# Second feed-forward of a two-layer attention block: the down product in three rounded parts, interleaved over four tiles

## The chip, the cores and the metric

The kernel runs on one core of a Trainium2 chip. Its engines are TensorE (PE: matmuls, with weight loads beside them), VectorE (DVE), ScalarE (ACT), GpSimd (POOL) and the DMA queues, here mostly issued by SyncE (SP). Each engine works through its own queue in order, and they wait for each other by semaphores. The metric is the device time of one execution in microseconds (us), the median of several runs.

## The reference, cut to what matters

`x` is 16 x 64 rows of 256 columns. Four residual stages follow one another: banded attention, a feed-forward on the chosen half of the rows, a cross attention with 32 query and 8 key heads, and the second feed-forward, which is the one that the change is about:

```python
def _L1_ffn_ref(hidden_states, gate_w, up_w, down_w, expert_weight, ln_gamma, ln_beta):
    logits = jnp.einsum('bsh,he->bse', hidden_states, gate_w)          # 8 logits
    routing_weights, selected_experts = jax.lax.top_k(logits, 2)
    h = jnp.einsum('bsh,hi->bsi', hidden_states, up_w)                 # 256 -> 1024
    h = jnp.square(jax.nn.relu(h))
    shared_out = jnp.einsum('bsi,ih->bsh', h, down_w)                  # 1024 -> 256
    y = shared_out + (hidden_states @ expert_weight) * routing_weights.sum(axis=-1, keepdims=True)
    mu = y.mean(axis=-1, keepdims=True)
    var = jnp.mean(jnp.square(y - mu), axis=-1, keepdims=True)
    return (y - mu) * jax.lax.rsqrt(var + EPS) * ln_gamma + ln_beta
x = x + _L1_ffn_ref(_layernorm(x), ...)
```

All is float32.

## The kernel before, in words

The 1024 rows are eight tiles of 128. The last part of the program, from the second half of the first feed-forward to the end of the cross attention, is written by hand as slots, `slot1(n)` for n from -18 to 53: every engine has a function of that name, and `at(n, first, step, count)` says which index of a job falls to slot n. Within a slot an engine does its jobs in the order of the code. Cross attention scores fall to slots 0 to 31 (L628), one (tile, quarter) a slot; the exponentials (L998 on ACT) and their products follow five and more slots later. A tile t of the attention ends with the output product at slot 14 + 4t (L684), its add into `x` on DVE at 15 + 4t (L1415), statistics at 17 + 4t, POOL's inverse deviation (`inv_std`, L1055 and L1058: add and power) and DVE's normalisation (L1209) at 18 + 4t, PE's transposes at 20 + 4t (L731) and the two halves of the normalised tile at 21 + 4t: a rounded copy on ACT (L992) and the rest, DVE's subtraction from it (L1384). With high and low halves of both operands a float32 product is made of three one-pass products (type fp32r): high x high, high x low, low x high. A plain float32 product is recorded as two instructions and takes more passes.

The second feed-forward works on halves of four tiles (512 rows). For each of 8 chunks f of the hidden width:
- PE `moe_up(half, f)` (L752): six fp32r products of 512 columns into bank `S[m % 2]`, m = 8 half + f. Called an up block below.
- ACT `moe_relu(m)` (L1015): relu from the bank into one of two buffers.
- the square: DVE `moe_square` (L1462) in the first half, POOL (L1193) in the second, into `hT`.

For each tile: PE's gate block (L771), six fp32r products of 264 columns for the expert product and the logits; DVE's top-two and their sum (L1468, L1470); ACT's scaling by that sum, `moe_scale` (L1024); PE's down product (L777), eight float32 products of 256 columns into a bank of `ST`, tile after tile; then on DVE, in `moe_out`, one behind another: the add (L1473), two statistics instructions (L1204, L1206), subtract the mean and multiply (L1477), wait for POOL's add and power (L1055, L1058), and the last multiply and add (L1482); SP stores the tile. POOL adds the residual and beta (L1184) in the tail.

In the first half, up blocks fall to slots 35 to 42, relu and square to 36 to 43, gate and down products to 44 to 51, half a tile a slot; `MOE_OUT` puts the closing of tiles 0 to 2 in slots 46, 48 and 53. After the slots PE does up blocks 8 to 15 and then gate and down product for tiles 4 to 7; DVE does `moe_out` for tiles 3 to 7.

The weights `up` and `down` (1 MB each) come with the other late loads at the start. ACT casts `up` into its high half at slots 29 to 32 (L977) and POOL subtracts (L1154) at 30 to 33; the gate weights follow at 37 and 38 (L980, L1157).

Of the kernel before, what the change touches and what calls it, by code (L numbers as in the profile page):

```python
# [23 lines left out]
P = 128  # L24
# [5 lines left out]
DF = 1024  # L30
# [18 lines left out]
def build(nc, a):  # L49
    ctx = ExitStack()  # L50
    with ctx:
# [6 lines left out]
        def sem(name):  # L58
# [36 lines left out]
        up = sb("up", [P, 2, DF])  # L95
        down = sb("down", [P, FC, T])
# [56 lines left out]
        names = ("ld_first ld_ctx ld_ctx2 ld_w0 ld_b0 ld_ident act_w0 pool_w0 act_part pe_part dve_part ld_small ld_x1 ld_x ld_rest ld_late st_out "  # L153
# [7 lines left out]
                 "h_ln h_rstd h_xn hp_xT ha_xT hl_xT ha_w hpool_w hpool_up h_xb hp_up ha_up h_up hp_dn hp_eg h_tk h_moe h_ln2 h_rstd2 h_y h_out").split()  # L161
# [75 lines left out]

        def stacked(p, i):

            return r32(q1[:, p % 3, :, :, :, i, :].rearrange("p g t b q -> p g (t b) q"))  # L240
# [12 lines left out]
        MOE_OUT = {46: 0, 48: 1, 53: 2}  # L253
# [58 lines left out]
        def _(sp):  # L312
            def load(dst, src, name):
# [28 lines left out]
                    (up[:, :, :], a["up"].rearrange("(k p) f -> p k f", p=P)),  # L342
                    (down[:, :, :], a["down"].rearrange("(k p) f -> p k f", p=P)),
                    (eg[:, :, 0:T], a["ew"].rearrange("(k p) f -> p k f", p=P)),
                    (eg[:, :, T:T + NEXP], a["gw"].rearrange("(k p) f -> p k f", p=P))]
            assert len(late) == 9
# [14 lines left out]
        LATE = 16 * 9  # L361
# [3 lines left out]
        def _(pe):  # L365
# [235 lines left out]
            def slot1(n):  # L601
# [154 lines left out]
            def moe_down(t, f0, f1):  # L756

                half, m = divmod(t, 4)
                if f0 == 0:
                    if t == 0:  # L760
                        pe.wait_ge(s["ga_o"], TILES)
                        pe.wait_ge(s["ga_ex"], 4 * TILES)
                    if t == 1:
                        pe.wait_ge(s["ga_hq"], PAIRS)
                        pe.wait_ge(s["g_lq"], PAIRS)
                    if t >= 2:
                        pe.wait_ge(s["h_y"], 2 * t - 3)
                    if t == 0:
                        pe.wait_ge(s["hpool_w"], 5)
                    for i, (k, a, b) in enumerate(PARTS):  # L770
                        last = mm((O, PJ)[t % 2][:, 0:T + NEXP], r32(xq[half][:, m, b, k, :]), r32(eg2[:, a, k, :]),  # L771
                                  start=(i == 0), stop=(i == len(PARTS) - 1))
                    last.then_inc(s["hp_eg"], 1)
                for f in range(f0, f1):
                    if m == 0:
                        pe.wait_ge(s["hpool_up" if half else "h_up"], f + 1)
                    last = mm(ST[t % 2][:, 0:T], hT[:, f, P * m:P * m + P], down[:, f, :], start=(f == 0), stop=(f == FC - 1))  # L777
                if f1 == FC:
                    last.then_inc(s["hp_dn"], 1)
# [12 lines left out]
        def _(act):  # L792
# [145 lines left out]
            def slot1(n):  # L938
# [31 lines left out]
                t = MOE_OUT.get(n)  # L970
                if t is not None:
                    moe_scale(t)
                i = at(n, 29, 1, 4)
                if i is not None:
                    act.wait_ge(s["gp_st"], 24)
                    k, c = divmod(i, 2)
                    nc.scalar.copy(r32(up2[:, 0, k, 512 * c:512 * c + 512]), up[:, k, 512 * c:512 * c + 512]).then_inc(s["ha_w"], 1)  # L977
# [620 lines left out]
```

## Time and profile before

| | |
|---|---|
| median of 3 runs | 342.35 us (341.98 to 342.72) |
| the profiled execution | 340.92 us |
| its span, first to last instruction | 339.2 us |
| PE busy | 307.2 us, 91% |
| PE weight loads | 239.0 us, 70% |
| DVE busy | 236.2 us, 70% |
| ACT busy | 199.6 us, 59% |
| POOL busy | 181.8 us, 54% |
| mean granted TensorE clock | 0.998 |

The profile is of one execution; times in it count from its first instruction. Busy times are of engines, and weight loads lie beside matmuls. A line such as L752 is a line of the kernel before. The chain is what ended last, followed back step by step to what released each step. The granted clock is the share of 2.4 GHz that PE was given. Matmuls are pipelined, so one that is recorded with 0.38 us can follow another after 0.22: counts over a stretch are read, not single durations.

### The profile page before, as it was taken

How to read it: one execution, taken by the hardware profiler on the slowest of the kernel's cores; microseconds unless marked ns; L12 is line 12 of the kernel's file. 1: busy time of each engine (PE TensorE's matmuls, PEld its weight loads, DVE VectorE, ACT ScalarE, POOL GpSimd, SP SyncE). 2: the span in 40 equal slices, each digit the busy share in tenths (PEclk: the TensorE clock that was granted, in tenths of full speed). 3: DMA queues.
4: the chain of work that ended last, by engine and by line, in shares of the span. 5: the costliest groups of instructions: out<-in, count | busy, mean ns of one | idle time of the engine just before them, and what ended most of it. 6: DMA issues, size and time to landing. Idle time of an engine off the chain costs nothing.

```text
span 339.2 us, 7193 instructions
## 1 busy us (share of the span) xinstructions
PE 307.2 (91%) x2166; PEld 239.0 (70%) x2166; DVE 236.2 (70%) x921; ACT 199.6 (59%) x414; POOL 181.8 (54%) x294
## 2 busy tenths in 40 slices
PE   1987999999999999999898998869899999999993
PEld 1966667777676767776587886647567677988892
DVE  6777788999999998984526346665788746661264
ACT  3757987878787888777640334376778953113210
POOL 5667565676785946585712712453342822335643
PEclk9999999999999999999999999999999999999999
DMA  7999010101010110100000000000000000000000
GB/s 188 366 371 332 3 44 7 46 3 41 12 33 15 25 25 19 32 2 4 2 0 0 0 2 0 0 2 1 2 1 2 0 2 0 3 31 15 18 31 31
DMA packets 13301, 14.51 MB, mean 43 GB/s; under 512 B 2512, under 2 KB 11984, under 8 KB 13264
## 3 DMA queue, kind: packets, MB, share of 16 engines
q1 hardware_dynamic: 12688, 13.72, 13.0%
q8 instruction: 19, 0.31, 0.4%
q10 hardware_dynamic: 576, 0.33, 0.3%
q14 instruction: 18, 0.15, 0.1%
HBM read 10.64 MB, written 1.05 MB: 34 GB/s over the span
## 4 chain that ended last, share of the span: by engine, by line
PE 61%; DVE 17%; issue 8%; ACT 6%; POOL 5%; DMA 1%; SPq 0%; POOLq 0%; DVEq 0%; ACTq 0%
PE S L752 6%; PE S L418 6%; PE O L445 5%; PE ST L429 4%; DVE masked L1251 4%; PE ST L777 4%; PE S L554 4%; PE S L628 2%; PE S L695 2%; PE PJ L672 2%; PE O L709 2%; PE XB L527 2%; PE PJ L383 2%; PE PJ L393 2%; PE XB L684 2%
## 5 line engine op out<-in xcount | busy, mean ns | idle before, releaser
L1251 DVE CUSTOM_DVE_ANT_0 masked<-S,band 128x192 bf16<-128x192 f32 x256 | 80.3, 353 | 14.1 <-PE S L418 13.0
L870 ACT ACTIVATE ex<-ST 128x384 f32<-128x384 f32 x128 | 61.4, 489 | 14.6 <-PE ST L429 12.6
L1055 POOL TENSOR_SCALAR rstd<-mv 128x1 f32<-128x1 f32 x40 | 12.0, 301 | 79.9 <-DVE mv L1206 79.8
L418 PE MATMUL S<-qk 128*128 128x384 f32 x128 | 53.4, 417 | 0.1
L429 PE MATMUL ST<-qk 128*128 128x192 f32 x256 | 47.7, 269 | 2.2 <-ACT ex L870 1.9
L429 PEld LDWEIGHTS ST<-qk 128*128 128x128 f32 x256 | 45.0, 189 | 4.5 <-issue 3.5
L1113 POOL TENSOR_SCALAR_AFFINE_SELECT ex<-ex 128x512 f32<-128x512 f32 x32 | 21.3, 665 | 30.3 <-ACT ex L870 30.1
L418 PEld LDWEIGHTS S<-qk 128*128 128x128 f32 x128 | 24.1, 188 | 17.3 <-issue 15.3
L445 PE MATMUL O<-ex,v 128*32 128x192 f32 x512 | 34.1, 338 | 0.0
L1393 DVE TENSOR_REDUCE mw<-S 128x8 f32<-128x512 f32 x32 | 21.9, 686 | 13.0 <-PE S L628 13.0
L840 ACT ACTIVATE hs<-PJ,sb,byhead 128x512 fp32r<-128x512 f32 x29 | 22.6, 779 | 12.5 <-PE PJ L384 12.0
L777 PE MATMUL ST<-down,hT 128*128 128x256 f32 x128 | 28.9, 379 | 0.0
L777 PEld LDWEIGHTS ST<-down,hT 128*128 128x128 f32 x128 | 23.8, 190 | 2.9
L1058 POOL TENSOR_TENSOR rstd<-rstd,given 128x1 f32<-128x1 f32 x40 | 23.0, 575 | 3.3
L752 PE MATMUL S<-qk 128*128 128x512 f32 x96 | 24.3, 402 | 0.0
L998 ACT ACTIVATE ex<-ST 128x512 f32<-128x512 f32 x32 | 19.1, 597 | 6.9 <-PE ST L641 6.3
L1251 DVE DVE_READ_ACCUMULATOR2_ANT mw<- 128x1 f32 x256 | 21.1, 82 | 0.0
L1015 ACT ACTIVATE cxT<-S 128x512 f32<-128x512 f32 x16 | 9.6, 598 | 19.4 <-PE S L752 19.4
L752 PEld LDWEIGHTS S<-qk 128*128 128x128 f32 x96 | 17.7, 188 | 4.3 <-issue 0.4
L1140 POOL TENSOR_TENSOR qk<-kp,kmask 128x512 fp32r<-128x512 f32 x16 | 16.5, 1056 | 7.7 <-PE ST L641 4.0
L1110 POOL TENSOR_SCALAR_AFFINE_SELECT ex<-ex 128x512 f32<-128x512 f32 x32 | 20.5, 642 | 0.0
L383 PE MATMUL PJ<-xs,w0h 128*128 128x256 f32 x58 | 18.2, 335 | 1.8 <-issue 1.5
(200 smaller groups left out, 709.2 us busy)
## 6 DMA issues: line engine op xcount, KB each, us to landing
qk<-kp SPq DMA_DIRECT2D x48, 48.0 KB
w<-in_w SPq DMA_DIRECT2D x2, 1024.0 KB, 10.0
cx<-in_cx SPq DMA_DIRECT2D x1, 1024.0 KB, 9.2
up<-in_up SPq DMA_DIRECT2D x1, 1024.0 KB, 11.6
down<-in_down SPq DMA_DIRECT2D x1, 1024.0 KB, 11.6
out<-x SPq DMA_DIRECT2D x8, 128.0 KB, 1.7
cxT<-in_cxT SPq DMA_DIRECT2D x1, 768.0 KB, 6.7
x<-in_x SPq DMA_DIRECT2D x1, 768.0 KB, 8.5
```

The source lines that it names most:

```text
L383: mm(bank[:, T * b:T * b + T], r32(w0h[:, n, :]), r32(xs[:, b, :]), start=True, stop=False)
L418: mm(out, r32(qp[:, t % 2, g, b, P * c:P * c + P]), r32(mv_), start=True, stop=True).then_inc(s["pe_s"], 1)
L429: last = mm(ST[n % 2][:, WIN * h:WIN * h + WIN], r32(kb[:, t % 2, g, 2 * w + h, b, P * c:P * c + P]), r32(qp[:, t % 2, g, b, BAND * c:BAND ...
L445: last = mm(O[32 * j:32 * j + 32, BAND * c:BAND * c + WIN], v0f[:, t % 2, c, b, j, 16 * g:16 * g + 32], ex[:, (n // 2) % 4, j, :], start=( ...
L752: last = mm(S[m % 2][:, :].rearrange("p (t c) -> p t c", t=4), r32(up2[:, a, k, P * f:P * f + P]), r32(xq[half][:, :, b, k, :]), start=(i ...
L777: last = mm(ST[t % 2][:, 0:T], hT[:, f, P * m:P * m + P], down[:, f, :], start=(f == 0), stop=(f == FC - 1))
L840: A(r32(hs[:, m % 2, :]), proj_bank(t, n)[:, :], ACT.Identity, bias=sb0[:, n:n + 1], scale=part0[:, n // 2:n // 2 + 1])\
L870: A(ex[:, (n // 2) % 4, 2 * w:2 * w + 2, :], ST[n % 2][:, 0:2 * WIN].rearrange("p (h k) -> p h k", h=2), ACT.Exp, scale=SCALE).then_inc(s[ ...
L1058: G.tensor_tensor(rstd[:, t:t + 1], rstd[:, t:t + 1], cols[:, 2:3], ALU.pow).then_inc(s[done], 1)
L1113: G.affine_select(out=e[:, :, 0:128], in_=e[:, :, 0:128], compare_op=ALU.is_ge, fill=0.0, base=0, pattern=[[0, 4], [1, 128]], channel_mult ...
L1251: last = V.tensor_tensor_reduce(out=masked[:, n % 2, h, :], in0=S[n % 2][:, WIN * h:WIN * h + WIN], in1=band[:, c, :], scale=1.0, scalar=N ...
L1393: V.tensor_reduce(rows.rearrange("p (i c) -> p i c", i=2)[:, :, 0:4], S[0][:, :].rearrange("p (i j k) -> p i j k", i=2, j=4), AX, ALU.max) ...
```

## The change

It touches the second feed-forward alone.

- **Down product.** `down` is split into a rounded half and the rest (`down2`; ACT at slots 13, 17, 21, 25, POOL at 14, 18, 22, 26). Each chunk of hidden values is split too: ACT squares the relu into a rounded half, DVE squares it in full and subtracts the rounded half. They lie in a ring of four buffers made of older tensors. The product of a tile and a chunk is three fp32r products of 256 columns.
- **Chunk by chunk.** `moe_down(tiles, f)` does chunk f for four tiles side by side. In the first half it falls to slots 39 to 46, two tiles sharing a bank. In the second half chunks 0 to 3 lie between up blocks, and chunks 4 to 7 are done tile after tile; gate blocks are a function of their own.
- **Closing in three stages.** `moe_top`, `moe_sum`, `moe_out` of different tiles are interleaved on DVE, with slots of their own and a written order after the slots.
- **Loads.** `up` and `down` are loaded into the first feed-forward's weight tensors once those are free.
- **POOL.** The squares of the second half leave it; the additions of beta move from the tail to slots 19 + 4t.

```diff
-        up = sb("up", [P, 2, DF])
-        down = sb("down", [P, FC, T])
+        down2 = sb("down2", [P, 2, FC, T])
...
+        def h_part(b, m):
+            i = m % 4
+            if b:
+                return kp[:, i, :, :].rearrange("p b k -> p (b k)") if i < 2 else w0l[:, i - 2, :, :].rearrange("p a b -> p (a b)")
+            return spread[:, i, :, :].rearrange("p a b -> p (a b)") if i < 2 else hs[:, i - 2, :]
+        def moe_sum_bank(t):
+            return ST[t // 2][:, T * (t % 2):T * (t % 2) + T] if t < 4 else (XB, MT, ST[0], ST[1])[t - 4][:, 0:T]
+        def ring_free(m):
+            last = m - 4
+            if last == FC - 1:
+                return s["hp_dn"], 4
+            return s["hp_df"], last + 1 if last < FC else last
...
-        MOE_OUT = {46: 0, 48: 1, 53: 2}
+        MOE_SCALE = {46: 0, 47: 1, 52: 2}
...
+            sp.wait_ge(s["fp_up"], 2 * FC)
+            load(w1[:, :, :], a["up"].rearrange("(k p) f -> p k f", p=P), "ld_up")
+            sp.wait_ge(s["fp_dn"], 4)
+            load(w2[:, :, :], a["down"].rearrange("(k p) f -> p k f", p=P), "ld_down")
...
PE, in slot1
-                i = at(n, 44, 1, FC)
-                if i is not None:
-                    moe_down(i // 2, 4 * (i % 2), 4 * (i % 2) + 4)
+                f = at(n, 39, 1, FC)
+                if f is not None:
+                    moe_down(range(4), f)
+                t = at(n, 44, 1, 4)
+                if t is not None:
+                    moe_gate(t)
...
+            def moe_gate(t):
...
+                if t >= 2:
+                    pe.wait_ge(s["h_moe"], t - 1)
...
+            def moe_down(tiles, f):
+                m = FC * (tiles[0] // 4) + f
+                pe.wait_ge(s["h_up"], m + 1)
+                if m == 0:
+                    pe.wait_ge(s["hpool_d"], 4)
+                    pe.wait_ge(s["ga_ex"], 4 * TILES)
+                if m == FC:
+                    pe.wait_ge(s["g_x"], TILES)
+                    pe.wait_ge(s["h_y"], 8)
+                for t in tiles:
+                    rows = slice(P * (t % 4), P * (t % 4) + P)
+                    for i, (a, b) in enumerate(((0, 0), (1, 0), (0, 1))):
+                        last = mm(moe_sum_bank(t), r32(h_part(b, m)[:, rows]), r32(down2[:, a, f, :]),
+                                  start=(f == 0 and i == 0 and (t >= 4 or t % 2 == 0)), stop=(f == FC - 1 and i == 2), skip_group_check=True)
+                    if f == FC - 1:
+                        last.then_inc(s["hp_dn"], 1)
+                if f < FC - 1 and len(tiles) == 4:
+                    last.then_inc(s["hp_df"], 1)
...
PE, after the slots
-            for f in range(FC):
-                moe_up(1, f)
-            for t in range(4, TILES):
-                moe_down(t, 0, FC)
+            second = range(4, TILES)
+            for f in range(3):
+                moe_up(1, f)
+            for f in range(3, FC):
+                if f < 7:
+                    moe_down(second, f - 3)
+                else:
+                    moe_gate(4)
+                moe_up(1, f)
+            moe_gate(5)
+            for t in second:
+                for f in range(4, FC):
+                    moe_down((t,), f)
+                if t + 2 < TILES:
+                    moe_gate(t + 2)
...
ACT
+                i = at(n, 13, 4, 4)
+                if i is not None:
+                    act.wait_ge(s["ld_down"], 16)
+                    nc.scalar.copy(r32(down2[:, 0, 2 * i:2 * i + 2, :]), w2[:, 2 * i:2 * i + 2, :]).then_inc(s["ha_d"], 1)
...
             def moe_relu(m):
                 act.wait_ge(s["hp_up"], m + 1)
                 if m >= 2:
+                    act.wait_ge(s["h_sq"], m - 1)
                 A(relu(m), S[m % 2][:, :], ACT.Relu).then_inc(s["ha_up"], 1)
+                if m == 0:
+                    act.wait_ge(s["gp_e"], 4 * PAIRS)
+                if m >= 4:
+                    act.wait_ge(*ring_free(m))
+                act.wait_ge(s["ha_up"], m + 1)
+                A(r32(h_part(0, m)), relu(m), ACT.Square).then_inc(s["ha_hi"], 1)
...
             for m in range(FC, 2 * FC):
                 moe_relu(m)
-                if m == FC + 3:
+                if m == FC:
                     moe_scale(3)
             for t in range(4, TILES):
                 moe_scale(t)
...
POOL
+                i = at(n, 14, 4, 4)
+                if i is not None:
+                    pool.wait_ge(s["ha_d"], i + 1)
+                    fs = slice(2 * i, 2 * i + 2)
+                    G.tensor_tensor(r32(down2[:, 1, fs, :]), w2[:, fs, :], down2[:, 0, fs, :], ALU.subtract).then_inc(s["hpool_d"], 1)
+                t = at(n, 19, 4, TILES)
+                if t is not None:
+                    pool.wait_ge(s["g_x"], t + 1)
+                    if t == 0:
+                        pool.wait_ge(s["fp_dn"], 4)
+                    G.tensor_tensor(with_beta(t), x[:, t, :], vecs[:, 4, :], ALU.add).then_inc(s["h_xb"], 1)
...
+            for t in range(TILES):
                 inv_std(t, "h_ln2", 2 * t + 2, "h_rstd2")
...
DVE
+                if n in (46, 47, 51):
+                    moe_top({46: 0, 47: 1, 51: 2}[n])
+                if n in (48, 50):
+                    moe_sum((n - 48) // 2)
+                if n in (49, 51):
+                    moe_out((n - 49) // 2)
...
+                V.tensor_tensor(squared(m), relu(m), relu(m), ALU.mult).then_inc(s["h_sq"], 1)
+                dve.wait_ge(s["ha_hi"], m + 1)
+                dve.wait_ge(s["h_sq"], m + 1)
+                if m == 0:
+                    dve.wait_ge(s["gpool_k"], 2 * TILES)
+                V.tensor_tensor(r32(h_part(1, m)), squared(m), h_part(0, m), ALU.subtract).then_inc(s["h_up"], 1)
...
-            for t in range(3, TILES):
-                moe_out(t)
+            moe_square(FC)
+            moe_sum(2)
+            moe_top(3)
+            moe_out(2)
+            moe_square(FC + 1)
+            moe_sum(3)
+            moe_out(3)
+            for m in range(FC + 2, 2 * FC):
+                moe_square(m)
+            moe_top(4)
+            moe_top(5)
+            for t in range(4, TILES):
+                moe_sum(t)
+                if 6 <= t + 2 < TILES:
+                    moe_top(t + 2)
+                if t >= 5:
+                    moe_out(t - 1)
+            moe_out(TILES - 1)
```

`moe_top(t)` is the top-two and their sum; `moe_sum(t)` waits for the scaled expert product and the tile's down product and does the add, the statistics and the subtract-and-multiply (it signals `h_y` after the add and after the last); `moe_out(t)` waits for POOL's power and does the last step.

## Rows read from the trace of the kernel before

**Rows 1.** The page's chain that ended last, shares by engine

```profile
PE 61%; DVE 17%; issue 8%; ACT 6%; POOL 5%; DMA 1%; SPq 0%; POOLq 0%; DVEq 0%; ACTq 0%
```

**Rows 2.** Windows: us, busy us (instructions) of each engine, granted clock, DMA share, GB/s

```profile
core 0: us, PE busy (x) PEld busy (x) DVE busy (x) ACT busy (x) POOL busy (x), PEclk, DMA share, GB/s
240.00:250.00 10.00, 8.81 (x69) 6.08 (x68) 7.90 (x17) 6.58 (x13) 5.57 (x7) 1.00 0.01 2
...
316.50:333.20 16.70, 16.70 (x89) 14.81 (x87) 8.57 (x23) 2.02 (x4) 8.97 (x15) 1.00 0.08 25
333.20:339.20 6.00, 0.11 (x1) 0.00 (x0) 2.32 (x8) 0.47 (x1) 1.08 (x2) 0.90 0.13 44
```

**Rows 3.** The chain in order of time, 260 to 340 us: start, us, what

```profile
276.50 0.22 PE XB L678 x2
276.72 0.57 PE O L709 x8
...
288.70 0.73 PE O L771 x6
289.43 3.45 PE ST L777 x16
...
297.29 0.74 PE O L771 x6
...
305.66 9.58 PE S L752 x42
...
318.34 0.68 POOL on L1184
```

**Rows 4.** Timeline of PE, 270 to 340 us: start, us, engine, line, what

```profile
296.90 0.38 PE L731 MATMUL MT<-ident,xn 128*128 128x128 f32 x2
...
305.31 11.28 PE L752 MATMUL S<-qk 128*128 128x512 f32 x48
...
329.70 3.62 PE L777 MATMUL ST<-down,hT 128*128 128x256 f32 x16
```

**Rows 5.** Timeline of DVE, 286 to 340 us; in brackets idle time and its releaser

```profile
332.43 0.84 DVE L1482 SCALAR_TENSOR_TENSOR x<-yr,rstd,on 128x256 f32<-128x256 f32 x1 [0.86 <-POOL rstd L1058]
333.20 0.16 DVE L1468 MAX8 tk<-PJ 128x8 f32<-128x8 f32 x1
333.39 0.16 DVE L1470 TENSOR_TENSOR rk<-tk 128x1 f32<-128x1 f32 x1
334.09 0.42 DVE L1473 TENSOR_TENSOR yr<-ST,onT 128x256 f32<-128x256 f32 x1 [0.54 <-ACT onT L1024]
...
335.01 0.18 DVE L1206 BATCH_NORM_AGGREGATE mv<-st 128x2 f32<-128x6 f32 x1
335.23 0.48 DVE L1477 SCALAR_TENSOR_TENSOR yr<-yr,mv,vecs 128x256 f32<-128x256 f32 x1
336.58 0.48 DVE L1482 SCALAR_TENSOR_TENSOR x<-yr,rstd,on 128x256 f32<-128x256 f32 x1 [0.86 <-POOL rstd L1058]
```

**Rows 6.** Timeline of ACT, 286 to 340 us

```profile
307.09 0.60 ACT L1015 ACTIVATE cxT<-S 128x512 f32<-128x512 f32 x1 [5.23 <-PE S L752]
...
333.58 0.47 ACT L1024 ACTIVATE onT<-PJ,rk 128x256 f32<-128x256 f32 x1 [3.67 <-DVE rk L1470]
```

**Rows 7.** Timeline of POOL, 286 to 340 us

```profile
332.27 0.72 POOL L1184 TENSOR_TENSOR on<-x,vecs 128x256 f32<-128x256 f32 x1
```

**Rows 8.** Weight loads of the gate block: ns min/median/max, first and last start

```profile
L771 PEld LDWEIGHTS O<-qk x24: 187/188/192, 288.4 to 325.3; 128*128 128x128 f32 x24
```

**Rows 9.** Groups by form, 180 to 340 us, ACT, POOL, DVE: busy us, mean ns

```profile
L977 ACT CAST qk<-up 128x512 fp32r<-128x512 f32 x4 | 2.5, 616 | 0.0
L992 ACT CAST qk<-MT 128x256 fp32r<-128x256 f32 x8 | 3.0, 372 | 0.8 <-PE MT L731 0.7
...
L1154 POOL TENSOR_TENSOR qk<-up,qk 128x512 fp32r<-128x512 f32 x4 | 5.1, 1273 | 2.9 <-ACT qk L977 2.9
...
L1462 DVE TENSOR_TENSOR hT<-cxT 128x512 f32<-128x512 f32 x8 | 5.5, 687 | 0.0
```

**Rows 10.** DMA issues: KB, median us from issue to landing

```profile
down<-in_down SPq DMA_DIRECT2D x1, 1024.0 KB, 11.6
```

**Rows 11.** Score products of slots 0 to 31: ns, first and last start us

```profile
L628 PE MATMUL S<-qk x64: 278/283/472, 208.1 to 265.1; 128*128 128x256 f32 x64
```

More of the change, by code:

```diff
@@ L754, in moe_up @@
                 last.then_inc(s["hp_up"], 1)
-            def moe_down(t, f0, f1):
+            def moe_gate(t):
                 half, m = divmod(t, 4)
[L759 to L779, printed above, removed]
@@ new lines, in moe_gate @@
+                if t == 0:
+                    pe.wait_ge(s["ga_o"], TILES)
+                    pe.wait_ge(s["hpool_w"], 5)
+                if t == 1:
+                    pe.wait_ge(s["ga_hq"], PAIRS)
+                    pe.wait_ge(s["g_lq"], PAIRS)
+                if t >= 2:
+                    pe.wait_ge(s["h_moe"], t - 1)
+                for i, (k, a, b) in enumerate(PARTS):
+                    last = mm((O, PJ)[t % 2][:, 0:T + NEXP], r32(xq[half][:, m, b, k, :]), r32(eg2[:, a, k, :]),
+                              start=(i == 0), stop=(i == len(PARTS) - 1))
@@ new lines, in moe_gate @@
+                last.then_inc(s["hp_eg"], 1)
+            def moe_down(tiles, f):
[16 more added lines that the diff above has]
+                    last.then_inc(s["hp_df"], 1)
@@ L1153, in slot1 @@
                     cs = slice(512 * c, 512 * c + 512)
[L1154 removed]
+                    G.tensor_tensor(r32(up2[:, 1, k, cs]), w1[:, k, cs], up2[:, 0, k, cs], ALU.subtract).then_inc(s["hpool_w"], 1)
+                i = at(n, 14, 4, 4)
[6 more added lines that the diff above has]
+                    pool.wait_ge(s["g_x"], t + 1)
+                    if t == 0:
+                        pool.wait_ge(s["fp_dn"], 4)
+                    G.tensor_tensor(with_beta(t), x[:, t, :], vecs[:, 4, :], ALU.add).then_inc(s["h_xb"], 1)
                 if n == 38:
@@ L1174, in _ @@
                 slot1(n)
-            def moe_norm(t):
-                pool.wait_ge(s["g_x"], t + 1)
-                if t == 0:
-                    pool.wait_ge(s["gp_bt"], TILES)
-                if t >= 2:
-                    pool.wait_ge(s["h_out"], t - 1)
-                G.tensor_tensor(on[:, t % 2, :], x[:, t, :], vecs[:, 4, :], ALU.add).then_inc(s["h_xb"], 1)
-                inv_std(t, "h_ln2", 2 * t + 2, "h_rstd2")
-            for t in range(3):
-                moe_norm(t)
-            for f in range(FC):
-                pool.wait_ge(s["ha_up"], FC + f + 1)
-                if f == 0:
-                    pool.wait_ge(s["hp_dn"], 4)
-                G.tensor_tensor(hT[:, f, :], relu(FC + f), relu(FC + f), ALU.mult).then_inc(s["hpool_up"], 1)
-            for t in range(3, TILES):
-                moe_norm(t)
+            for t in range(TILES):
+                inv_std(t, "h_ln2", 2 * t + 2, "h_rstd2")
         @block.vector
@@ L1470, in moe_out, with moe_sum @@
                 V.tensor_tensor(rk[:, t:t + 1], tk[:, t % 2, 0:1], tk[:, t % 2, 1:2], ALU.add).then_inc(s["h_tk"], 1)
+            def moe_sum(t):
+                y, scaled = moe_rows(t)
                 dve.wait_ge(s["h_moe"], t + 1)
-                dve.wait_ge(s["hp_dn"], t + 1)
-                V.tensor_tensor(yr[:, 0, :], ST[t % 2][:, 0:T], onT[:, t % 2, :], ALU.add).then_inc(s["h_y"], 1)
+                dve.wait_ge(s["hp_dn"], t + 1 if t >= 4 else t + 2 - t % 2)
+                if t == 1:
+                    dve.wait_ge(s["gp_bt"], TILES)
+                V.tensor_tensor(y, moe_sum_bank(t), onT[:, t % 2, :], ALU.add).then_inc(s["h_y"], 1)
                 dve.wait_ge(s["h_y"], 2 * t + 1)
-                stats(t, yr[:, 0, :], "h_ln2", 2 * t)
+                stats(t, y, "h_ln2", 2 * t)
                 dve.wait_ge(s["h_ln2"], 2 * t + 2)
-                V.scalar_tensor_tensor(out=yr[:, 1, :], in0=yr[:, 0, :], scalar=mv[:, t, 0:1], in1=vecs[:, 3, :],
+                V.scalar_tensor_tensor(out=scaled, in0=y, scalar=mv[:, t, 0:1], in1=vecs[:, 3, :],
                                        op0=ALU.subtract, op1=ALU.mult).then_inc(s["h_y"], 1)
+            def moe_out(t):
                 dve.wait_ge(s["h_y"], 2 * t + 2)
@@ L1486, in _ @@
                 slot1(n)
-            for t in range(3, TILES):
-                moe_out(t)
+            moe_square(FC)
[16 more added lines that the diff above has]
+            moe_out(TILES - 1)
 def constants():
```

30 lines of the change are left out of this document (15 added, 15 removed).

## Prediction

> **What bounds the kernel now.** I read the page's chain first: TensorE (PE) holds 61% of the chain that ended last, VectorE (DVE) 17% [rows 1]. Then the windows: from 316.5 to 333.2 us, the second half of the second feed-forward, PE has no idle time at all, at a granted clock of 1.00, its level of 2.4 GHz [rows 2]. The chain in order of time says what it does there: a gate block of six matmuls takes 0.74, a tile's sixteen half-passes of the fp32 down product 3.45, and 42 matmuls of the up product 9.58, so 1.37 for an up block of six [rows 3]. From 318.34 on the chain leaves PE: the closing steps of tile 3 and then of tiles 4 to 7 run one behind another on DVE, ScalarE (ACT) and POOL, about 4.14 a tile. That is as long as PE's gate and down work for a tile (0.74 + 3.45), so neither leads by much: PE's last matmul ends at 333.32 [rows 4], the last tile's sum starts on DVE at 334.09 [rows 5].
>
> The last tile also gives the price of the closing steps [rows 5 to 7]. Top-two: 333.20 to 333.55, 0.35. ACT's scaling: 0.47. Stage "sum" (add, two statistics, subtract and multiply): 334.09 to 335.71, 1.62. POOL's variance and power, from the statistics' end to the last step's start: 1.39. Last step: 0.48. From PE to ACT it takes about 0.4 beyond the block: the up block that starts at 305.31 leaves PE after 1.37 and its relu starts at 307.09 [rows 4, 6].
>
> **The down product.** Removed: 64 fp32 products of 256 columns, 8 tiles x 3.45 = 27.6. Added: 192 one-pass products of 256 columns. No such product is in this stage; the nearest is the gate block, 264 columns with new weights each time, 0.74 / 6 = 0.123 [rows 3]. By columns that is 0.118 to 0.12. A chunk (four tiles, three parts) is then 12 x 0.118 = 1.42, sixteen chunks 22.7. Bounds: the array could take them at 256 / 264 of the best pitch in a gate block (0.12), so hardly under 22; from above, if each waited out its weight load of 0.188, as the loads of the gate blocks take [rows 8], 36. I take 22.7, since in the gate block the same loads lie beside the matmuls. **Term: -4.9.**
>
> **The parts of the hidden values.** For each of 16 chunks ACT gets a Square beside its relu (0.60 more) and DVE a square and a subtraction (two of 0.69 [rows 9]) where it had one, or none in the second half. POOL loses eight squares. In the steady state a round is an up block and a down chunk, 2.8 on PE, against 1.4 on DVE and 1.2 on ACT: hidden. At slot 37 it isn't: ACT must pass relu 1, Square 1, the cast of the gate weights, a copy for the second norm and the copy that the output product of tile 6 waits for. That is 0.4 + 0.6 + 0.6 + 0.62 + 0.37 + 0.37 = 3.0 behind up block 1, and PE has 0.22 + 0.57 + 1.37 = 2.2 to do [rows 3, 6, 9]; without the Square the same sum gives a lag of 0.2. **+0.6.**
>
> **Half one to half two.** Now PE's transposes for tile 7 (at 296.90) stand between a down product and a gate block [rows 4], so the copy and the lower part that follow are covered. Afterwards nothing stands between them and up block 8: 0.4 + ACT 0.37 + DVE 0.42 (its add of the same size) [rows 5, 9]. **+1.2.** Call the start of up block 8 U.
>
> **The new wait.** The first down chunk of half two waits for h_y >= 8, stage sum of tile 3, on PE, and every later matmul is queued behind it. If nothing held PE, it would come after three up blocks, at U + 4.1. DVE's queue from U on is written out by the change: last step 0 (0.48), sum 1 (1.62), top 2 (0.35), last step 1 (waits about 0.45 for POOL's 1.39, then 0.48): U + 3.4. Square pair 8 needs relu 8, which on ACT is queued behind the scaling of tile 2, which waits for top 2: relu 8 ends at U + 3.65, the pair at U + 5.05. Sum 2: 6.65. Top 3: 7.0. Last step 2: 7.95. Relu 9 stands on ACT behind the scaling of tile 3, which waits for top 3: it ends at U + 8.15, the pair at U + 9.5, sum 3 at U + 11.1. PE meanwhile does up 8 and 9, waits 0.8 for relu 8, does up 10 until U + 5.0 and then idles 6.1. **11.1 - 4.1 = +7.0.** PE is the bound again afterwards (2.8 a round against 1.4), so it is not earned back.
>
> **The clock.** In the last window, with PE done at 333.3 and the span ending at 339.2, the mean granted clock is 0.90 [rows 2]: over 6.0 us that is 1.2 us at the lower level, 1.2 GHz, so after the end of its work the engine had idled some 4.7 us when it fell. In the new wait it idles 6.1, so I expect it to restart at the lower level. How long it stays there no row shows. Bounds: 0, and 21, if all the remaining 21 us of PE work ran at half rate. I take the first round after the wait, a down chunk and an up block, 2.8 us of work, the smallest whole unit of what comes next, since no row speaks for more. **+2.8.**
> The Trainium skill, TensorE: Matmul & The Clock Gate, section on the HAM clock gate, says that the clock of the array is either 1.2 or 2.4 GHz, that it falls after idle time and is given back after sustained work; an estimate by that page would put the loss at about 1.5 to 3.5 us. By that rule, the trace agrees that it falls (0.90), and does not show that it rises.
>
> **The end.** Behind up block 15 PE has gate 5 and nine down products, 1.8; relu, square and subtraction take 0.4 + 0.6 + 0.7 + 0.7 = 2.4: wait 0.6. Gate block 6 waits for the scaling of tile 4, whose top is queued behind the last subtraction: 0.35 + 0.5 against 0.35 of PE: wait 0.5. **+1.2** with the handovers. In the last tiles PE delivers every 2.15 and then 1.42, DVE needs 1.62 + 0.48, with a top 2.45: it lags by about 1.5 at the last tile where it lagged 0.9. POOL's adds no longer stand there, so the last step takes 0.48, not the 0.84 that it takes beside POOL's 0.72 (332.43 beside 332.27) [rows 5, 7]. **+0.5.**
>
> **Attention stage.** New there are four casts on ACT (0.62, as L977), four subtractions on POOL (1.27, as L1154 [rows 9]) and eight additions on POOL (0.72, moved from the tail). The stage removes nothing, so it can't gain; at most every cast and half of POOL's work shows, about 4. In its window ACT is idle a third of the time and POOL nearly half [rows 2]. I take 0.4, near the end at nothing, since four casts in 22 slots stand beside that idle third. The two loads of 1 MB move behind the first feed-forward: 11.6 to land [rows 10], and the down cast stands ten slots later, a slot being (265.1 - 208.1) / 31 = 1.8 [rows 11]: 18 us. Nothing, and SP's queue has only the stores behind it. **+0.4.**
> What a POOL instruction does to one of DVE is the 0.84 against 0.48 above. The Trainium skill, SBUF — State Buffer, section on who shares ports, says that a tensor_tensor of DVE with both inputs in SBUF waits out a GpSimd instruction that reads SBUF; the new square pairs are of that kind, so by it the pairs of slots 36 to 43 would wait up to 0.7 beside each of POOL's four long ones there, some 2 us of DVE work, still under PE's 2.8 a round.
>
> **Sum.** -4.9 + 0.6 + 1.2 + 7.0 + 2.8 + 1.2 + 0.5 + 0.4 = +8.8. The profiled execution took 340.92 (span 339.2), the median of the runs is 342.35, 1.4 more; I set the same difference on the median: 351.1 (span about 348.0).
>
> **Rivals.**
> 1. The clock stays, or is back at once: 348.3. For it: 6.1 is only 1.4 longer than the one fall seen. 0.27.
> 2. The other side: PE never waits for stage sum 3, because DVE gets through its list by the time PE reaches the chunk; it decides from the point where sum 3 ends before U + 5.0 instead of 11.1. Relu 8 comes in time too, and there is no fall of the clock: -4.9 + 0.6 + 1.2 + 1.2 + 0.5 + 0.4 = -1.0, 341.3. Against it: DVE's own instructions between U and there are 2 x 0.48 + 3 x 1.62 + 2 x 0.35 + 4 x 0.69 = 9.3 us of busy time, waits not counted. 0.05.
> 3. The attention stage pays in full: ACT's casts delay Exp, and DVE waits at POOL's port: +3.6, 354.7. For it: ACT, PE and DVE alternate in the chain there. 0.08.
> 4. The one-pass products go at the weight load's 0.19: 192 x 0.188 = 36 for 22.7, 13 more, 364. Against it: the gate block's 0.123. 0.03.
> 5. The change doesn't do what it says: the later loads or the ring of four buffers stall PE so that it isn't about the closing steps at all; each Square waits for the chunk four back, 0.4 after PE has done it. Near no change by chance: 0.02.
> The forecast itself has 0.55.
>
> **Numbers.** A measurement of this kernel can tell 0.2%, 0.7 us, from no change. Slower by more: the forecast and rivals 1, 3, 4, 0.93; same is rival 5, 0.02; faster is rival 2, 0.05. The range reaches down past rival 1 (348.3), with the attention stage free and the end and the chunks cheaper by a microsecond or two, to 346, and up to rival 3, 354.7; outside are rivals 2, 4 and 5 and what lies further towards the clock's upper bound.
>
> **What would show it.** In the profile after: down products at a pitch near 0.12; the chunk line of PE with one idle stretch of about 6 us, released by DVE's subtract-and-multiply of stage sum, right after up block 10; an ACT relu of block 9 behind a scaling; a granted clock under 1.00 just behind it; the transposes of tile 7 followed by a gap of about 1.2; attention slots of 1.8 as before. It is wrong if PE is dense from 280 us to the end, or if S L628 spans over 60 us instead of 57.

## The result, and the profile after

The changed kernel takes 349.23 us (median of 4 runs, 348.81 to 349.34) where the kernel before takes 342.17 beside it: ratio 1.0201, 95% interval 1.0182 to 1.022. On another occasion it was 349.72 against 342.58, 1.0217 (1.019 to 1.0244). It is slower by 7.1 us; 8.8 had been forecast.

The page of the changed kernel: busy times, the granted clock in 40 slices, the chain's shares.

```profile
PE 306.8 (88%) x2230; PEld 240.1 (69%) x2230; DVE 251.6 (72%) x945; ACT 211.4 (61%) x434; POOL 180.3 (52%) x290
...
PEclk9999999999999999999999999999999999996998
...
PE 59%; DVE 20%; issue 9%; ACT 6%; POOL 4%; DMA 1%; SPq 0%; POOLq 0%; DVEq 0%; ACTq 0%
```

PE works no longer than before (306.8 us against 307.2), but in a longer span. One slice has a clock of 0.6, where the kernel before had nines throughout. The timeline of PE, 278 to 348 us (start, us; in brackets idle time and what ended it), shows where the time goes; line numbers are now those of the changed kernel. L786 is the up block, L819 the down product, L802 the gate block, L762 the transposes for the second norm, L683 those of the attention's output:

```profile
286.69 0.63 PE L683 MATMUL XB<-ident,osb 128*128 128x128 f32 x4 [0.56 <-DVE x L1476]
...
305.67 0.38 PE L762 MATMUL MT<-ident,xn 128*128 128x128 f32 x2
306.98 3.01 PE L786 MATMUL S<-qk 128*128 128x512 f32 x12 [0.92 <-DVE qk L1445]
310.18 1.65 PE L786 MATMUL S<-qk 128*128 128x512 f32 x6 [0.19 <-ACT cxT L1076]
317.65 0.77 PE L819 MATMUL XB<-down,spread 128*128 128x256 f32 x2 [5.82 <-DVE on L1552]
...
320.35 1.68 PE L786 MATMUL S<-qk 128*128 128x512 f32 x6
321.87 0.40 PE L819 MATMUL XB<-down,spread 128*128 128x256 f32 x2
...
323.28 1.55 PE L786 MATMUL S<-qk 128*128 128x512 f32 x6
...
334.78 0.50 PE L819 MATMUL XB<-down,hs 128*128 128x256 f32 x2 [0.43 <-DVE w0l L1531]
...
335.56 0.99 PE L802 MATMUL O<-qk 128*128 128x264 f32 x6 [0.17 <-ACT onT L1091]
```

Right behind up block 10 PE idles 5.82 us until DVE's subtract-and-multiply of tile 3. The chunk behind it takes 317.65 to 320.35, 2.70 us; the next takes 321.87 to 323.28, 1.41. The up block between them takes 1.52, others 1.39. The windows give the clock (columns as in [rows 2]):

```profile
311.80:314.00 2.20, 0.03 (x1) 0.00 (x0) 1.52 (x6) 0.51 (x2) 1.08 (x2) 0.95 0.00 0
314.00:316.00 2.00, 0.00 (x0) 0.00 (x0) 1.86 (x4) 1.82 (x4) 0.00 (x0) 0.50 0.19 66
316.00:317.60 1.60, 0.00 (x0) 0.00 (x0) 1.40 (x4) 0.38 (x1) 0.51 (x1) 0.50 0.00 0
317.60:320.30 2.70, 2.65 (x12) 2.68 (x13) 1.78 (x3) 0.00 (x0) 0.57 (x1) 0.50 0.17 52
320.30:323.00 2.70, 2.70 (x18) 2.45 (x17) 0.30 (x1) 0.84 (x2) 0.00 (x0) 0.94 0.02 3
```

0.95 over 2.20 us is 0.22 us at the lower level (1.2 GHz): the clock fell at about 313.8, 2 us after PE's last matmul, and rose shortly after 320.3. What DVE and ACT did in the wait, from their timelines:

```profile
309.71 0.48 DVE L1560 SCALAR_TENSOR_TENSOR x<-on,rstd,hT 128x256 f32<-128x256 f32 x1 [0.58 <-POOL rstd L1125]
310.15 0.69 DVE L1526 TENSOR_TENSOR cxT<-cxT 128x512 f32<-128x512 f32 x1
310.95 0.69 DVE L1531 TENSOR_TENSOR kp<-cxT,spread 128x512 fp32r<-128x512 f32 x1
...
313.29 0.16 DVE L1539 TENSOR_TENSOR rk<-tk 128x1 f32<-128x1 f32 x1
314.04 0.48 DVE L1560 SCALAR_TENSOR_TENSOR x<-yr,rstd,hT 128x256 f32<-128x256 f32 x1 [0.58 <-POOL rstd L1125]
314.48 0.69 DVE L1526 TENSOR_TENSOR cxT<-cxT 128x512 f32<-128x512 f32 x1
...
317.02 0.48 DVE L1552 SCALAR_TENSOR_TENSOR on<-on,mv,vecs 128x256 f32<-128x256 f32 x1
```

```profile
313.49 0.47 ACT L1091 ACTIVATE onT<-PJ,rk 128x256 f32<-128x256 f32 x1 [2.64 <-DVE rk L1539]
313.86 0.59 ACT L1076 ACTIVATE cxT<-S 128x512 f32<-128x512 f32 x1
```

Up block 9 ended before 310, but its relu (313.86) stands on ACT behind the scaling of tile 3 (313.49), which waits for the top of tile 3 (313.29), itself in DVE's list behind the square pair 8 (310.15, 310.95) and the sum of tile 2.

The profiled execution's span is 8.3 us longer, 1.2 more than the medians are apart. In its first 13 us it falls behind by 1.6: the first product of `w0l` into `ST` started at 11.68 before and at 13.29 here. In a second profile of the same changed kernel it started at 12.06, in those of the experiments between 11.67 and 13.71. So this shift is not the change's, and it covers the 1.2.

### The profile page after: what moved, and what is told of

Read it like the earlier page. It is cut to its first block, busy times and chain, and to the rows that moved or that the text cites. A ratio compares the mean times of both kernels' runs of the same rounds, so it can differ in the third digit from the quotient of the medians.

```text
span 347.5 us, 7389 instructions
## 1 busy us (share of the span) xinstructions
PE 306.8 (88%) x2230; PEld 240.1 (69%) x2230; DVE 251.6 (72%) x945; ACT 211.4 (61%) x434; POOL 180.3 (52%) x290
## 4 chain that ended last, share of the span: by engine, by line
PE 59%; DVE 20%; issue 9%; ACT 6%; POOL 4%; DMA 1%; SPq 0%; POOLq 0%; DVEq 0%; ACTq 0%
PE S L449 6%; PE O L476 5%; PE ST L460 4%; DVE masked L1312 4%; PE S L786 4%; PE S L585 4%; PE ST L819 4%; PE S L659 2%; PE PJ L703 2%; PE S L726 2%; PE XB L558 2%; PE PJ L414 2%; DVE st L1265 2%; PE PJ L424 2%; DVE mw L1454 2%
## 5 line engine op out<-in xcount | busy, mean ns | idle before, releaser
L786 PE MATMUL S<-qk 128*128 128x512 f32 x96 | 25.5, 404 | 1.1 <-DVE qk L1445 0.9
L1125 POOL TENSOR_TENSOR rstd<-rstd,given 128x1 f32<-128x1 f32 x40 | 24.2, 605 | 3.3
L786 PEld LDWEIGHTS S<-qk 128*128 128x128 f32 x96 | 17.4, 191 | 5.6 <-DVE qk L1445 1.2
L659 PE MATMUL S<-qk 128*128 128x256 f32 x64 | 15.4, 322 | 3.0 <-DVE mw L1454 1.8
L1175 POOL TENSOR_SCALAR_AFFINE_SELECT ex<-ex 128x256 f32<-128x256 f32 x32 | 13.3, 416 | 8.3 <-ACT ex L926 8.0
```

Source lines behind the costliest of these rows:

```text
L659: last = mm(S[0][:, T * ii:T * ii + T], r32(q1[:, (t // 2) % 3, g, t % 2, b, 2 * ii:2 * ii + 2, :]), r32(k1[:, t % 4, g, b, :, :]), start= ...
L786: last = mm(S[m % 2][:, :].rearrange("p (t c) -> p t c", t=4), r32(up2[:, a, k, P * f:P * f + P]), r32(xq[half][:, :, b, k, :]), start=(i ...
L1125: G.tensor_tensor(rstd[:, t:t + 1], rstd[:, t:t + 1], cols[:, 2:3], ALU.pow).then_inc(s[done], 1)
```

## The experiments

Theory: the first down chunk of half two waits on PE for the end of tile 3's stage sum, which a written order puts late; the wait costs once more through the clock; the three-part product alone is a gain. Rivals: the order does not matter, or the loss lies elsewhere. Ratios are to the kernel before; the changed kernel's is 1.0201 and 1.0217.

**Order alone.** Tops and sums before the square pair on DVE, the last step of tile 1 taken out of slot 51 for it; on ACT the scaling of tile 3 stands ahead of the loop, before relu 8:

```diff
+            moe_scale(3)
             for m in range(FC, 2 * FC):
                 moe_relu(m)
-                if m == FC:
-                    moe_scale(3)
...
-            moe_square(FC)
-            moe_sum(2)
             moe_top(3)
+            moe_out(1)
+            moe_sum(2)
+            moe_sum(3)
+            moe_square(FC)
             moe_out(2)
             moe_square(FC + 1)
-            moe_sum(3)
             moe_out(3)
```

> The changed kernel, with DVE's and ACT's order after the slots altered alone: tops and stage sums of tiles 2 and 3 before the square pair of block 8, and the scaling of tile 3 before relu 8. Theory (the first down chunk of half two waits behind DVE's written order, and only there): DVE reaches the end of stage sum 3 about 6.5 us after up block 8 starts and the square pair 8 after 7.9 instead of the measured 10.7, so PE's wait of 5.8 shrinks to about 2.7 to 3.0 and the kernel takes 2.8 us less, 346.4; if the clock no longer falls in the shorter wait, up to 4.1 less, 345.1. Rival (the loss is in the down products themselves or in the attention stage, and the wait would open anyway): no change, 349.2.

345.2 us, ratio 1.0076 (1.0057 to 1.0096): 4.0 to 4.5 us less than the changed kernel, the outer end of what was expected. Its PE timeline and windows:

```profile
314.85 0.50 PE L819 MATMUL XB<-down,spread 128*128 128x256 f32 x2 [2.52 <-DVE kp L1530]
```

```profile
312.30:314.85 2.55, 0.03 (x2) 0.01 (x1) 2.38 (x6) 0.92 (x3) 1.67 (x3) 1.00 0.00 0
314.85:317.50 2.65, 2.65 (x17) 2.46 (x18) 2.54 (x5) 0.56 (x1) 0.00 (x0) 1.00 0.15 49
```

The chunk starts 2.8 earlier, the wait is 2.52, and in this profile the clock did not fall. The order is the cause; no instruction was added or removed. What ends the wait now is the square pair of block 8, which stands last in the new order.

**The add only.**

```diff
                 if m == FC:
-                    pe.wait_ge(s["h_y"], 8)
+                    pe.wait_ge(s["h_y"], 7)
```

> The changed kernel, but the first down chunk of half two waits only for the add of tile 3 (h_y >= 7), which is what frees the bank, and not for the step after its statistics (h_y >= 8). Theory: the add ends 1.2 us before that step, so PE's wait is 4.6 instead of 5.8 and the kernel takes 1.2 less, 348.0; the chunk itself is still done at the lower clock. Rival (PE is released by something else that comes just as late, such as the square pair): no change, 349.2.

347.68, ratio 1.0165 (1.0144 to 1.0187), 1.2 to 2.0 less by ratios and medians; PE's wait reads 4.62 for 5.82. It is this semaphore that holds PE. The three steps behind the add were waited for without need: what the chunk needs is the bank, and it is the add that reads it.

**Filler.** The same wait, with PE kept busy:

```diff
                 if m == FC:
                     pe.wait_ge(s["g_x"], TILES)
+                    pe.wait_ge(s["hl_xT"], TILES)
+                    for _ in range(44):
+                        mm(MT[:, 0:T], r32(down2[:, 0, 0, 0:P]), r32(down2[:, 0, 1, :]), start=True, stop=True, skip_group_check=True)
                     pe.wait_ge(s["h_y"], 8)
```

> The changed kernel, with 44 one-pass products of 256 columns into a free bank put in front of the first down chunk of half two, 44 x 0.118 = 5.2 us of work inside a wait of 5.8. Nothing is waited for less, only PE is kept busy. Theory (the wait costs once more through the clock): the granted clock stays at 1.00, the chunk behind the wait takes 1.41 instead of 2.70, and the kernel takes 1.3 us less, 347.9. Rival (the clock is not what makes the chunk slow, or its fall costs nothing that counts): no change, 349.2; if the filler overruns the wait, some tenths more.

346.8, ratio 1.0138 (1.0117 to 1.0159): by the ratios 2.2 to 2.7 us gained by 44 matmuls whose results are thrown away. PE timeline and a window of it:

```profile
310.71 5.54 PE L817 MATMUL MT<-down 128*128 128x256 f32 x44
316.57 0.51 PE L822 MATMUL XB<-down,spread 128*128 128x256 f32 x2 [0.32 <-DVE on L1555]
```

```profile
316.60:319.20 2.60, 2.60 (x17) 2.42 (x18) 1.72 (x3) 0.00 (x0) 0.57 (x1) 1.00 0.15 50
```

The chunk now runs at 1.00. The gain is larger than what the first profiled execution had lost (1.3 in the chunk, 0.1 in the up block behind it), so that execution was a mild one. The other profiles of kernels with the wait show it: all have one stretch at the lower level, 6.8 us long in each, but it begins sooner or later in the wait, and so more or less of it falls on PE's work.

| profile | clock falls, us after PE's last matmul | PE's work at the lower level, us |
|---|---|---|
| changed kernel, first | 2.0 | 3.0 |
| add only | 2.0 | 4.3 |
| plain products in the changed kernel (below) | 2.3 | 3.3 |
| changed kernel, again | 4.0 | 5.0 |
| transposes earlier | 5.0 | 6.0 |
| beta later, alone | 5.0 | 6.0 |

Work at the lower level takes about twice its time (2.70 for 1.41), so half of the last column is an estimate of what each execution lost: 1.5 to 3.0 us. The filler's 2.2 to 2.7 lies inside that.

**The transposes of tile 7 earlier**, in slot 46 on PE, 47 on ACT and 48 on DVE:

```diff
-                t = at(n, 20, 4, TILES)
+                t = 7 if n == 46 else None if n == 48 else at(n, 20, 4, TILES)
```

> The changed kernel, with PE's transposes of tile 7, ACT's copy and DVE's lower part two, two and one slots earlier, so that chunk 7 and two gate blocks cover their handovers. The gap of 0.9 us in front of up block 8 goes. Theory (behind it DVE's list sets the pace, not PE): the list starts about 0.9 earlier too, since DVE had idled 1.1 in front of the lower part, so PE's chunk 8 comes 0.9 earlier: 348.3. Rival (the gap itself is hidden by the long wait behind it, DVE's list being what it is): no change, 349.2, and the wait grows to 6.7.

349.58, ratio 1.0218 (1.0197 to 1.0239). No gain: the rival's time holds, not the theory's. Its wait does not: the long one stays 5.82, and what had been gained in front of up block 8 is lost in front of up block 10, where PE waits 1.54 for relu 8 instead of 0.19. DVE's timeline tells why:

```profile
304.91 0.41 DVE L1548 TENSOR_TENSOR yr<-ST,onT 128x256 f32<-128x256 f32 x1
...
307.39 0.48 DVE L1560 SCALAR_TENSOR_TENSOR x<-yr,rstd,hT 128x256 f32<-128x256 f32 x1 [0.86 <-POOL rstd L1125]
```

Stage sum 0 now stands behind the lower part, and the last step of tile 0 comes so soon after it that DVE waits 0.86 for POOL. The idle time on DVE was not removed, only moved. In this profile the clock stayed low from 318 to 324 us, 0.50 in both windows:

```profile
318.00:321.00 3.00, 2.79 (x13) 2.82 (x14) 1.84 (x4) 0.00 (x0) 0.71 (x2) 0.50 0.14 46
321.00:324.00 3.00, 3.00 (x10) 2.42 (x10) 0.00 (x0) 0.29 (x1) 0.00 (x0) 0.50 0.01 3
```

**The changed kernel again**, beside the next three.

> The changed kernel once more, unaltered, on the chip and beside the runs of the kernel before that the next three share. Expected 349.2 as in the first runs, 2.0% above the kernel before. It also tells whether the opening of its first profile (1.6 us later than in the profile of before by 13 us, with matmuls at half rate for longer) belongs to the kernel: by theory it does not, and the shift at 13 us is anywhere between 0 and 1.6.

349.72 as said above; the shift at 13 us was 0.4, so the late opening is not the kernel's.

**The wait taken apart.**

```diff
                 if m == FC:
                     pe.wait_ge(s["g_x"], TILES)
-                    pe.wait_ge(s["h_y"], 8)
+                    pe.wait_ge(s["hl_xT"], TILES)
                 for t in tiles:
+                    if m == FC and t in (6, 7):
+                        pe.wait_ge(s["h_y"], {6: 3, 7: 6}[t])
...
             moe_square(FC)
-            moe_sum(2)
             moe_top(3)
-            moe_out(2)
-            moe_square(FC + 1)
-            moe_sum(3)
-            moe_out(3)
+            moe_sum(2, "add")
+            moe_sum(3, "add")
+            moe_out(0)
+            moe_sum(2, "rest", 6)
+            moe_out(1)
+            moe_square(FC + 1)
+            moe_sum(3, "rest", 6)
+            moe_out(2)
+            moe_square(FC + 2)
+            moe_out(3)
```

The add and the rest of stage sum are called apart for tiles 2 and 3; the top of tile 2 and the sum of tile 1 stand in slots 50 and 51 with no last step among them, the scaling of tile 2 in slot 51 and that of tile 3 behind relu 9, and the transposes are early.

> The changed kernel with the wait taken apart: each tile of the first down chunk of half two waits only for the adds that free its own bank (tiles 4 and 5 for none, tile 6 for tile 1's, tile 7 for tile 3's), DVE does top 2, stage sum 1, square pair 8, top 3 and the two adds of tiles 2 and 3 before anything else of the closing steps, the scaling of tile 3 stands behind relu 9, and the transposes of tile 7 are early as in the run that moved them alone. Theory: PE is dense from 287 us to the last chunks; the 5.8 us in front of the chunk, the 1.3 lost to the clock, the 0.9 in front of up block 8 and the 0.2 behind it all go: 349.2 - 8.2 = 341.0, just under the kernel before (342.3). Rival (closing steps that are put off come back as waits for DVE in the rounds behind, or at the end): 343 to 345. Rival (nothing but the order after the slots counted, and the rest of the loss is elsewhere): 345.2, as with the sums first.

341.3, ratio 0.997 (0.9957 to 0.9983): 8.4 us less than the changed kernel beside it, and 0.3% faster than the kernel before. PE was not dense: 1.25 us of waiting came up in front of the second chunk, for the pair of block 9. That the theory's 341.0 was met all the same is partly luck: it had no such wait, and it counted 1.3 for the clock, where the filler gave 2.2 to 2.7. Four things were altered together (PE's waits, DVE's order, ACT's order, the transposes); how the 8.4 divides among them was not measured, except that order alone had given 4.0 to 4.5.

**Additions of beta later**, in that kernel and alone in the changed one:

```diff
-                t = at(n, 19, 4, TILES)
+                t = {44: 5, 45: 6, 47: 7}.get(n, at(n, 19, 4, 5))
```

> The kernel of the run before, and POOL's additions of beta for tiles 5, 6 and 7 moved from slots 39, 43 and 47 to 44, 45 and 47. Theory (in slots 38 and 39 two POOL additions back to back hold up first DVE's normalisation, 0.82 for 0.41, and then the square pair, 1.22 for 0.69, and PE waits 0.56 for what follows them): the square takes 0.69 and PE's wait of 0.56 in front of the transposes of tile 7's attention goes: 0.5 less than the run before, 340.5. Rival (POOL's additions do not delay DVE there): no change to the run before.

340.85, ratio 0.9956 (0.994 to 0.9972); on another occasion 340.63, 0.9944 (0.9928 to 0.996).

> The changed kernel with only the additions of beta for tiles 5, 6 and 7 moved, as in the run before. Theory: PE's wait of 0.56 goes, and since the first half is paced by PE, all that follows comes 0.5 earlier: 348.7. Rival (the wait is not POOL's doing): 349.2.

349.3, ratio 1.0205 (1.018 to 1.023). Both are 0.4 less than their neighbours, the size of the theory and within the intervals. The traces are plainer. DVE's and POOL's timelines of the changed kernel:

```profile
283.45 0.82 DVE L1270 TENSOR_SCALAR xn<-x,mv,rstd 128x256 f32<-128x256 f32 x1 [0.46 <-POOL rstd L1125]
284.19 1.22 DVE L1526 TENSOR_TENSOR cxT<-cxT 128x512 f32<-128x512 f32 x1
```

```profile
283.39 0.73 POOL L1232 TENSOR_TENSOR hT<-x,vecs 128x256 f32<-128x256 f32 x1
284.08 0.78 POOL L1241 TENSOR_TENSOR yr<-x,vecs 128x256 f32<-128x256 f32 x1
```

and DVE's with the addition moved, in the faster kernel:

```profile
284.50 0.68 DVE L1526 TENSOR_TENSOR cxT<-cxT 128x512 f32<-128x512 f32 x1
```

The square takes 0.68 where it took 1.22, and PE's wait of 0.56 is gone in both kernels. The normalisation still takes 0.82 to 0.83, since POOL's other addition now runs beside it.

**Plain float32 products** in the same order, one for the three (`mm(bank, h_part(0, m)[:, rows], w2[:, f, :])`); the low half is left out of them. First in the changed kernel, then in the fastest so far:

> The changed kernel with its order and waits, but each tile and chunk takes one plain float32 product of the rounded half with the unsplit weights in place of three one-pass products (the low half of the hidden values is still made and waited for, and is left out of the product). It measures the term of the down product alone. Theory: a chunk of four tiles takes 4 x 0.43 = 1.72 us of PE instead of the 1.41 of the trace, sixteen chunks 4.9 more; the chunks of half one and of the rounds behind the wait are all on PE's path, so 349.3 + 4.9 = 354.2, less some tenths where PE had waited for DVE at the end. Rival (the plain product is no dearer here): 349.3. Rival (PE is not the bound in half the places): about 351.8.

352.76, ratio 1.03 (1.0272 to 1.0328): 3.0 more than the changed kernel's 349.7, not 4.9. The profile says 4.0, if both are counted from the first product of `w0l` into `ST` (at 11.67 here); they have nearly the same PE work at the lower clock, 3.3 and 3.0 us. A chunk takes 1.73 for 1.41, 5.1 in all, and waits for DVE cover the rest: 0.3 in slot 39 (from chunk 0 to the transposes 2.12, with one-pass products 2.13), 0.3 at block 15 (from up block 15 to the first product of tile 5 5.38 and 5.37) and 0.5 in the tail (5.5 behind PE's end for 5.97).

> The same exchange in the kernel that had all waits taken apart and the additions of beta moved. Again the low half of the hidden values is left out of the product. Theory: the three-part product is what the change gains, and in this kernel it is gained in full, so with plain products it takes 340.9 + 4.9 = 345.8 less the 1.2 that PE still waits for the pair of block 9, which the longer chunk covers in part: 344.8 to 345.8, more than the kernel before. Rival (the gain of this kernel over the one before comes from the closing steps): it stays under 342.4.

344.54, ratio 1.0069 (1.0038 to 1.01): 3.7 more, and slower than the kernel before. So it is the product that makes this kernel faster than the one before; with plain products the change does not pay, even in the best order. What the order alone is worth was not measured: the hidden values are still split here, which is work on ACT and DVE that a plain product doesn't need. This profile shows a surprise in the attention stage. PE timeline and windows:

```profile
227.91 0.70 PE L726 MATMUL S<-hs,spread 128*128 128x512 f32 x2 [1.70 <-ACT qk L1071]
```

```profile
226.00:228.00 2.00, 0.30 (x3) 0.12 (x3) 0.69 (x1) 1.72 (x4) 2.00 (x3) 1.00 0.00 0
228.00:230.00 2.00, 2.00 (x10) 1.63 (x10) 1.11 (x2) 0.60 (x1) 0.39 (x1) 0.68 0.00 0
230.00:232.00 2.00, 2.00 (x14) 1.14 (x14) 0.17 (x1) 0.79 (x2) 0.00 (x0) 0.50 0.00 0
```

The clock fell at 228.7, 0.8 us after PE had gone on working, and the stretch at the lower level is 3.4 us long. In the profile of before, PE idles the same 1.70 us in front of this product and the clock stays at 1.00.

**Pair 9 first.** In the kernel with beta moved:

```diff
             moe_sum(3, "add")
+            moe_square(FC + 1)
             moe_out(0)
             moe_sum(2, "rest", 6)
             moe_out(1)
-            moe_square(FC + 1)
-            moe_sum(3, "rest", 6)
-            moe_out(2)
             moe_square(FC + 2)
+            moe_sum(3, "rest", 6)
+            moe_out(2)
             moe_out(3)
```

> The kernel with the waits taken apart and the additions of beta moved, and DVE's square pair of block 9 in front of the last steps of tiles 0 and 1 and the statistics of tile 2, not behind them. Theory (PE's remaining wait of 1.24 us in front of the second down chunk is that pair's place in DVE's list, and the steps put off fit into the rounds behind): the wait goes and the kernel takes 1.2 less than the 340.9 of the run before it, 339.7. Rival (the statistics of tile 3, put off further, now hold up the pair of block 10 or 11 by as much): no change, 340.9.

340.89, ratio 0.9958 (0.9937 to 0.9978), the unaltered one beside it 340.63. No gain, as the rival had it. The wait of 1.26 went, and one of 0.84 came in front of the fourth chunk, for the pair of block 11:

```profile
318.51 0.50 PE L821 MATMUL XB<-down,hs 128*128 128x256 f32 x2 [0.84 <-DVE w0l L1531]
```

In the two profiles PE's end came 0.45 earlier, less than the runs can tell.

> The kernel with the waits taken apart and the additions of beta moved, unaltered, beside the run before. Expected 340.9 as before, 0.4% under the kernel before.

## Why the prediction was right, point by point

The measured time, 349.23, lies in the range (346.0 to 354.7), 1.9 under the number. By its steps, in the first profile; U is the start of up block 8. A loss of PE is read from start to start here, against the same work without a wait. That is more than the idle time in brackets, since a one-pass product is recorded with 0.28 us but the next one can start 0.12 behind its start.

| step | forecast | measured | where |
|---|---|---|---|
| down product | -4.9 | -5.0 | a chunk takes 1.41: 16 x 1.41 against 27.6 |
| slot 37 and attention | +0.6, +0.4 | +0.5 together | PE's shift against before grows from 1.6 at 13 us to 2.1 at slot 38 |
| POOL beside DVE, slot 39 | nothing | +0.7 | from chunk 0 (284.56) to the transposes (286.69) 2.13 for 1.41; 0.56 of it idle |
| half one to half two | +1.2 | +1.2 | from the transposes (305.67) to up block 8 1.31 for 0.14 |
| the new wait | +7.0 | +6.5 | chunk at U + 10.67, three up blocks take 4.17 |
| clock | +2.8 | +1.4 here, 2.2 to 2.7 by the filler | 2.70 for 1.41 and 1.52 for 1.39 |
| end | +1.2 | +1.1 | from up block 15 (331.02) to tile 5's product (336.39) 5.37 for 4.26 |
| tail | +0.5 | +0.1 | 5.97 after PE's end, 5.88 before |

The measured terms add up to 6.5, with the opening's 1.6 to 8.1 of the 8.3 by which the spans differ.

**The wait** stood where it was put, behind the list that was written out: forecast U + 11.1, measured U + 10.67. Up block 10 starts 0.4 late for the forecast 0.8, since relu 8 ends at U + 3.1 and not U + 3.65; the chunk then comes 6.1 later than up block 10 would have allowed, as forecast. That it was the order was shown by changing it alone.

**Half one to half two** is right as a term of the sum, PE's time up to U, but it is no cost of its own. The run with the gap removed says that nothing is gained: behind it DVE's list sets the pace. The forecast for that run had overlooked this.

**The end** came as forecast. **The tail** was 0.4 too dear: DVE was to lag by 1.5 at the last tile, but its last add starts 0.7 after PE's end (342.26 and 341.53).

**The clock** fell, as in [rows 2], but 2.0 to 5.0 us after PE's last matmul, and the cost is not one number: 1.5 to 3.0 by the profiles, 2.2 to 2.7 by the filler. The 2.8 that was taken lies near the upper edge of this. It came near by luck: it was the smallest unit of the work that comes next, and no row spoke for it.

**POOL's port** is a term that the sum put at nothing and that cost 0.7. The prediction said of the square pairs that they could be held up by up to 0.7 and hid it all under PE. The holding up was there, 1.22 for 0.69, but in slot 38 DVE's list has the add behind it that PE's next transposes wait for: a delay of DVE is hidden only if everything queued behind it is.

**The rivals.** That the clock stays (348.3) did not hold in any profile of the changed kernel, though its time is nearer to the measured 349.23 (0.9) than the forecast is (1.9): what the forecast put too high elsewhere (wait 0.5, slot 37 and attention 0.5, tail 0.4) is more than what it left out at POOL's port. The other side, PE never waiting, would have been 341.3 by the prediction; with the wait taken apart 341.3 was measured. That the numbers are equal is chance: the rival still had the 1.2 between the halves, which that run took out, and had no wait of 1.25 for the pair of block 9. The one-pass product at the pace of weight loads did not happen: 1.41 / 12 is 0.1175 us each.

## What to carry to other kernels

When an interleaved order is written by hand for several engines, follow each wait to the last item of the list in front of it, on the engine that it waits for and on the engine that waits: a wait for "all sums" behind a list of squares, tops and last steps cost more than the faster product gave back. Wait for what frees the resource (the add that reads the bank), tile by tile, and not for the end of the stage. Add up gaps along the path, not beside it: a gap in front of a longer wait, on an engine that doesn't set the pace there, was free here.

## What the runs showed of the hardware that was not expected

- The granted clock fell 4.7 us after PE's last matmul at the end of before, 2.0 to 5.0 us after it in the new wait of six profiles, and in the attention stage of one run 0.8 us after the end of an idle time of 1.7. It stayed through the same 1.70 in before and through 2.52 in the run with sums first. So with idle times of 1.7 to 2.5 us the clock was lost in one execution and kept in two.
- In all six profiles with the new wait the stretch at the lower level was 6.8 us long, whenever it began; in the attention stage it was 3.4. What it costs depends on how much of it falls on PE's work: 3.0 us of 6.8 in one, 6.0 in two others.
- A DVE product of one tile with itself, 0.69 alone, took 1.22 beside a POOL addition. The Trainium skill, SBUF — State Buffer, section "Who interferes with whom", says that a tensor_tensor with both inputs in SBUF contends with GpSimd's reads, and the trace agrees.
- In the first 13 us products of 256 columns go at one per 0.21 us and later at one per 0.12. The change from one to the other comes earlier or later: the same product starts at 13.29 in one profile of the changed kernel and at 12.06 in the other, between 11.67 and 13.71 in all, and PE's transposes in slot 39 are 1.2 apart in the two as well (286.69 and 285.49). The granted clock reads 1.00 there throughout, so the windows don't show it.
